# The next tile's layer norm ahead of the feature map in a linear-attention pass

## The reference

```python
# x = x + ln(attn(ln(x))); x = x + ln(ffn(ln(x)))
q, k, v = x @ Wq, x @ Wk, x @ Wv            # 16 heads of 64
qf = relu(q @ Wf + bf); kf = relu(k @ Wf + bf)
kv = einsum('blhf,blhd->bhfd', kf, v)       # summed over the whole sequence
out = einsum('blhf,bhfd->blhd', qf, kv)
out = out / max(einsum('blhf,bhf->blh', qf, kf.sum(1)), 1e-6)
attn = out @ Wo + bo
# ffn: silu(w1 x) * (w2 x) -> gelu(h1) -> gelu(h2) -> w3, 1024 -> 4096 -> 4096 -> 4096 -> 1024
```

## Time and profile before

| what | us |
|---|---|
| timed runs | 7970.59, 8002.57 (median 7986.58) |
| the profiled execution, its own time | 7969.23 |
| its span, slowest core | 7967.7 |
| cores' spans | 7951.3 to 7967.7, granted clock 0.856 to 0.859 |
| TensorE busy | 5975.1 (75%) |
| VectorE, ScalarE busy | 2174.3 (27%), 1708.7 (21%) |

### The profile page before, as it was taken

The page is one execution under the profiler, slowest core; times in us unless marked ns, Lnnn a source line. Parts: engine busy times, 40 slices in busy tenths (PEclk is TensorE's granted clock), DMA queues, the critical chain, the costliest instruction groups (busy, mean ns, idle before and its releaser), DMA issues.

```text
span 7967.6 us, 123239 instructions; the slowest of 8 cores (7951.3 to 7967.7 us)
## 1 busy us (share of the span) xinstructions
PE 5975.1 (75%) x50768; PEld 2892.6 (36%) x50768; DVE 2174.3 (27%) x3032; ACT 1708.7 (21%) x2637; POOL 207.9 (3%) x386
## 2 busy tenths in 40 slices
PE   4633447999993789999646334479999937899996
PEld 1311113445551344455323111234455513444553
DVE  2356544110103421011223565441101134210112
ACT  1211123211112331111112111332111123211111
POOL 0000000000000000000000000000000000000000
PEclk8665668999996899999866656789999968999998
DMA  3120012344442234444231200124444412344442
GB/s 70 35 61 22 11 53 54 73 77 75 77 97 60 52 61 80 76 75 78 66 80 43 53 21 11 53 54 78 77 75 77 97 56 54 64 77 76 77 76 73
DMA packets 97191, 503.12 MB, mean 63 GB/s; under 512 B 7360, under 2 KB 15744, under 8 KB 48512
## 3 DMA queue, kind: packets, MB, share of 16 engines
q0 software_dynamic: 68224, 394.56, 27.2%
q1 hardware_dynamic: 28416, 100.67, 3.6%
HBM read 856.11 MB, written 33.55 MB: 112 GB/s over the span
## 4 chain that ended last, share of the span: by engine, by line
PE 69%; DVE 16%; ACT 5%; DMA 5%; issue 4%; another core or an unknown queue 1%; DVEq 1%; ACTq 0%; POOL 0%; SPq 0%; POOLq 0%
PE psb L78 59%; PE psb L57 5%; PE psb L80 5%; DVE ltmp L100 4%; DMA wc<-w_t 3%; DVE normsb L128 3%; ACT sq L89 2%; ACT ltmp L89 1%; DVE xa L100 1%; DMA xpr<-xp_hbm 1%; DVE ltmp3B L100 1%; DVE a L114 1%; DMA xbf<-x 1%; DVE y L100 1%
## 5 line engine op out<-in xcount | busy, mean ns | idle before, releaser
L78 PE MATMUL psb<-a,wc 64*128 64x512 bf16 x10240 | 2226.4, 378 | 41.6 <-DVE a L114 29.6
L80 PE MATMUL psb<-a,wc 64*128 64x512 bf16 x10240 | 2226.5, 378 | 0.0
L78 PE MATMUL psb<-b,wc 64*128 64x512 bf16 x8192 | 1775.5, 377 | 12.3 <-ACT b L89 12.3
L80 PE MATMUL psb<-b,wc 64*128 64x512 bf16 x8192 | 1775.5, 377 | 0.0
L78 PEld LDWEIGHTS psb<-a,wc 64*128 64x128 bf16 x10240 | 965.7, 94 | 1154.9 <-issue 63.2
L78 PE MATMUL psb<-xnw,wc 64*128 64x512 bf16 x4096 | 961.1, 395 | 320.3 <-DMA wc<-w_t 257.0
L78 PEld LDWEIGHTS psb<-b,wc 64*128 64x128 bf16 x8192 | 771.5, 94 | 858.0 <-issue 21.8
L100 DVE TENSOR_TENSOR ltmp<-ltmp,psb 128x512 f32<-128x512 f32 x640 | 440.3, 688 | 2092.8 <-ACT ltmp L89 2042.8
L80 PEld LDWEIGHTS psb<-a,wc 64*128 64x128 bf16 x10240 | 966.7, 94 | 0.0
L80 PE MATMUL psb<-xnw,wc 64*128 64x512 bf16 x4096 | 961.8, 396 | 0.0
L89 ACT ACTIVATE ltmp<-psb 128x512 f32<-128x512 f32 x704 | 420.3, 597 | 2108.6 <-PE psb L80 2080.5
(11 more groups left out here) (118 smaller groups left out, 4065.1 us busy)
## 6 DMA issues: line engine op xcount, KB each, us to landing
wc<-h_t POOLq DMA_DIRECT2D x256, 1024.0 KB, 8.2
wc<-w_t POOLq DMA_DIRECT2D x96, 1024.0 KB, 8.4
xb<-x SPq DMA_DIRECT2D x16, 2048.0 KB, 9.4
xpr<-xp_hbm SPq DMA_DIRECT2D x16, 2048.0 KB, 13.7
xp_hbm<-xp SPq DMA_DIRECT2D x8, 2048.0 KB, 10.1
out<-outt SPq DMA_DIRECT2D x8, 2048.0 KB, 7.3
xbf<-x POOLq DMA_DIRECT2D x8, 1024.0 KB, 8.6
WA<-wk POOLq DMA_DIRECT2D x2, 2048.0 KB, 27.0
```

The costliest lines, as they stand in the source:

```text
L78: self.h.matmul(outA, lhsT[0:64, :], rhs[0:64, :], start=start, stop=stop, tile_position=(0, 0))
L80: ins = self.h.matmul(outB, lhsT[64:128, :], rhs[64:128, :], start=start, stop=stop, tile_position=(64, 0))
```

## The change

The part of a tile of pass 1 from the waits for its load up to the next `xbf` load's issue, squares and norm, becomes a function `p1_ln(tile)`. It is called once for tile 0 ahead of the loop, and in the loop for tile + 1 between V's and kf's text. The loop's head only takes over what the call returned. The kf stage moves from banks 6 and 7 to banks 4 and 5. Of the waits ahead of K, one `weave` and that on `gp` are left out; the load of `xb` stays at the end of the loop. Pass 2 and the feed-forward part are untouched.

```diff
@@ -463,7 +463,7 @@
-    for tile in range(seq_tiles):
+    def p1_ln(tile):
         j = tile
         b = j % 2
         xb = xbufs[b]
@@ -482,15 +482,20 @@
                     sq_ck=sq_ck, warm_bank=0,
                     save_to=(t["r_save"][:, tile * TT:(tile + 1) * TT],
                              t["mr_save"][:, tile * TT:(tile + 1) * TT]))
-        ve_xa = p.c["ve"]
         st["xbf_free"] = [("pe", p.c["pe"])]
         if j + 1 < seq_tiles:
             load_xbf(j + 1)
+        return {"tile": tile, "j": j, "b": b, "xal": xal, "ve_xa": p.c["ve"]}
+
+    pl = p1_ln(0)
+    for tile in range(seq_tiles):
+        j = pl["j"]
+        b = pl["b"]
+        xal = pl["xal"]
+        ve_xa = pl["ve_xa"]
 
         p.w("T", "dwA", st["wA_val"])
-        weave(p, bank_wait, 0, sn1["apply_ck"], per=4)
         p.w("T", "ve", ve_xa)
-        p.w("T", "gp", sn1["gp_end"])
         kql = [t["kq"][:, oc * TT:(oc + 1) * TT] for oc in range(NCH)]
         for oc in range(NCH):
             bA, bB = (0, 1) if oc % 2 == 0 else (2, 3)
@@ -543,9 +548,11 @@
                 st["l3_ve"] = p.c["ve"]
                 bank_consumed(bB)
 
+        pl = p1_ln(tile + 1) if tile + 1 < seq_tiles else None
+
         kf_se = [0] * NCH
         for c in range(NCH):
-            bk = 6 + c % 2
+            bk = 4 + c % 2
             bank_wait(bk)
             p.w("T", "se", se_k)
             for sub in range(4):
```

## The result

| | before | changed |
|---|---|---|
| profiled execution, its own time | 7969.23 | 7908.91 |
| span, slowest core | 7967.6 | 7907.3 |
| spans of the eight cores | 7951.3 to 7967.7 | 7891.2 to 7907.3 |
| lowest and median of all timed runs | 7970.59, 8109.85 (10 runs) | 7908.28, 8096.37 (11 runs) |

These took 7908 to 7910 us in the changed kernel and give a ratio of 0.991, with a 95% interval of 0.9887 to 0.9933. The change is worth 60 us of span, 0.8%: real, and well inside the 2% that decide between faster and no change.

A forecast was written before the change was run, and what follows sets the result against it. Hand-offs between engines, not TensorE's rate, were taken to bound the attention parts. Six boundaries (53.6) plus kf's banks (2.1) gave 55.7 us; from a base of 7980.8 the forecast was 7925, -0.7%, range 7880 to 7960.

The forecast's parts named there:

- the sum: Six pass 1 boundaries at 8.9 us less each, 53.6, plus 2.1 from kf's banks at two last tiles: 55.7 us.
- steps 1 to 6: New tile boundary from V to K: squares, statistics and row chain, broadcast, kf, apply beside kf, kv; K 8.9 us earlier.
- A: End of ScalarE's last eviction of V at a tile boundary, 124.46 in the profile before; the boundary's times count from it.
- The order in kf's favour: At the boundary kf waits for banks 4 and 5, not for the apply, which runs hidden beside kf (12.6 us).
- The bank edit: At each sequence's last tile kf no longer waits for V's last eviction: up to 1.06 us, twice, 2.1.
- three waits that fall away: The gp count and two weaves: said to cost nothing, their counts being zero or already reached.
- The clock in K: K was let start at the low clock in the new order too, rising 5.4 us after its start as before.
- the clock is lifted before K: Rival at the boundaries: kf at 0.16 pitch, K saves 2.7; 12.7 a boundary, 78 in all: 7903; chance 0.13.
- What follows moves forward: After each sequence's last tile, weights loaded after TensorE's last matmul just move forward; no loss was counted.
- VectorE ahead of kv: Slower rival: a late apply blocks kv's adds, delaying K beyond 1.7 us slack; 7991 at double pitch; either slower way 0.05.
- The f32 load: Slower rival: load late for the squares in 4 boundaries once landing takes 33.5 us, decides at 42; either slower way 0.05.
- The partly lost cover: Rival: apply slower beside kf and its evictions, or longer hand-over; down to half the gain left, 7935 to 7960; chance 0.07.

## Why the prediction was right or wrong, point by point

**The time: the step that failed is the base.** 7925 with 7880 to 7960 was forecast. The median over all eleven runs is 8096.4, outside; the executions that can be compared took 7908 to 7910, inside. The forecast took as its base the mean of three executions, 7980.8, none of them far from the fastest, and had no term for what lifts a median over many. The kernel before has a median of 8109.9 over ten runs, 129 us above that base; less the 55.7 of the sum that is 8054, outside the range too. So the change didn't cause the miss: the ratio of the two medians is 0.998. The same step cost 12 us even among the compared executions: the profiled one's own time, 7969.2, was the one to keep (six such executions of the kernel before lie at 7965 to 7971, three at 7980 to 8031), and gave 7913.5.

**Squares, statistics, chain, kf, kv (steps 1 to 6).** Right to some 0.2 us each: K's start was put at A + 38.4 and came at A + 38.8 (162.47 - 123.68); the broadcast, put at A + 18.7, came at A + 19.0. The squares stood uncovered with 6.73 us of idle, kf took 13.87, kv 5.07. The six boundaries were forecast at 53.6 and gave 53.0.

**The order in kf's favour.** Right, and shown by the kernel that keeps the old banks: the whole cover hangs on kf's banks.

**The bank edit.** Mechanism right, size off. The term was 1.06 us at the last tile; it measured 2.2 (4.4 for two), since kf, starting without a gap, keeps the high clock for 28 to 31 matmuls (4.5 to 4.9 us) instead of 8 to 11. The same omission hid that this edit alone is worth 26.5 us. The prediction speaks of three waits that fall away ahead of K, two of them weaves; the diff takes out one weave and the one on `gp`. Nothing hangs on it.

**The clock in K.** I let K have 5.4 us at the low clock in the new order, as the rows had it. It had 3.0 to 3.5 at all six boundaries, and the eight K stages took 6.7 us less in all. The rival "the clock is lifted before K" is wrong as well: kf and kv, without idle time, stayed at 0.50, and K started low. The truth lay between, and the kernel with idle time ahead of K says that it is not a fixed place. The Trainium skill's rule, that activity releases the throttle ("TensorE: Matmul & The Clock Gate", "What's actually happening"), agrees with the rise in K and is not borne out by kf, if busy time is taken for activity: TensorE is busy for 15.00 of 15 us there, at 0.50. What sets kf apart was not tested.

**What follows moves forward.** Not quite: 3.6 us were lost again outside pass 1. No term of the sum had them.

**The gain.** 55.7 was forecast, 60.3 measured: -0.6 from the boundaries, +2.3 from the bank edit, +6.7 from K, -0.2 between K and V, -3.6 from outside. That the sum came within 5 us is in part luck: K's clock and the loss outside, neither of them in the sum, have opposite signs.

**The rivals.** VectorE ahead of kv: slack forecast as 1.7, measured as about 1.5, and never used up. The f32 load: no wait for it appears at a boundary, the squares start 0.09 us after V's last eviction. The partly lost cover: the apply kept 0.79 us beside kf's evictions.

## What to carry to other kernels

Moving a chain of other engines' work ahead of a stage hides it only if the stage doesn't need what the chain holds, PSUM banks first of all: check the banks of both before pricing the order. Price what the move uncovers as well as what it covers, then look for gaps in a busy stage where the uncovered part fits; here the squares in V's gaps gave some 40 us more, beside the 60 of the change. Starting kf straight behind V instead of 1.06 us later saved 2.2 to 2.6 us a tile, since kf kept the high clock for longer.

## What the runs showed of the hardware

- kf, with TensorE busy for 15.00 of 15 us, stayed at the low clock for its whole 14 us where it started low. Where it followed V without a gap it started high and let the clock fall 2.5 to 5.9 us after its start.
- The rise in K came anywhere from 0.9 to 5.8 us after its start at the boundaries, and within one kernel it differed by up to 3.2 us. A forecast that counts the low stretch to a tenth is too fine by that much at each boundary.
- V, dense and at the high clock otherwise, took 15.7 instead of 14.0 us in some tiles, with a mean clock of 0.89, behind a K whose rise came early. A gain in K's clock can be lost again in V.
